# A two-block cross-attention kernel: the second block's context read from a kept transpose

## The reference, cut to what matters

```python
# first block, on x
x = attn(ln(x, g1, b1), ln(x, g1, b1), Wq1, Wk1, Wv1, Wo1, bo1) + x      # SELF
x = attn(ln(x, g2, b2), context, Wq2, Wk2, Wv2, Wo2, bo2) + x            # CROSS
x = geglu_ff(ln(x, g3, b3), Wp, bp, Wf, bf) + x                          # GEGLU
# second block
q, k, v = x @ Wq + bq, context @ Wk + bk, context @ Wv + bv              # CROSS2
out = softmax(q * 8**-0.5 @ k.T) @ v @ Wo + bo
out = out + gelu(ln(out) @ W1 + b1) @ W2 + b2                            # FFN
return x + out
```

## Time and profile before

| what | value |
| --- | --- |
| median of three runs | 463.78 us |
| lowest and highest run | 463.76 us, 464.13 us |
| profiled execution, its own time | 464.39 us |
| its span, first to last instruction | 462.7 us |
| TensorE matmul, weight load | 448.1 us (97%), 408.1 us (88%) |
| VectorE, ScalarE, GpSimd | 354.1, 322.5, 199.0 us |
| mean granted TensorE clock | 1.000 |

### The profile page before, as it was taken

One profiled execution on the slowest core, in us unless ns is written; L12 is line 12 of the kernel. 1 busy time (PEld: TensorE's weight loads), 2 busy tenths in 40 slices (PEclk: granted clock), 3 DMA queues, 4 the chain that ended last, 5 costly groups with the idle time before them and its releaser, 6 DMA issues.

```text
span 462.7 us, 17536 instructions
## 1 busy us (share of the span) xinstructions
PE 448.1 (97%) x7574; PEld 408.1 (88%) x7574; DVE 354.1 (77%) x642; ACT 322.5 (70%) x598; POOL 199.0 (43%) x219
## 2 busy tenths in 40 slices
PE   7989999999999999999999999999999999999897
PEld 6969898898998989989889899898999787777797
DVE  4899778778786787877877778696885678889572
ACT  5676776877778768877787777855545577776763
POOL 2584432555354634544353433531442232132583
PEclk9999999999999999999999999999999999999999
DMA  7102020310200000000000000000000000000011
GB/s 225 35 23 64 22 81 3 77 47 4 61 4 12 1 11 11 3 11 1 13 11 1 11 3 11 2 3 3 1 0 10 18 10 20 0 2 1 10 37 47
DMA packets 17301, 10.57 MB, mean 23 GB/s; under 512 B 7888, under 2 KB 16272, under 8 KB 17232
## 3 DMA queue, kind: packets, MB, share of 16 engines
q1 hardware_dynamic: 16800, 9.48, 7.4%
q10 hardware_dynamic: 432, 0.07, 0.1%
HBM read 8.50 MB, written 1.05 MB: 21 GB/s over the span
## 4 chain that ended last, share of the span: by engine, by line
PE 85%; DVE 9%; ACT 3%; issue 1%; DMA 1%; POOL 1%; DVEq 0%; SPq 0%
PE stage L606 12%; PE stage L608 11%; PE stage L607 11%; PE scp L697 7%; PE scp L772 7%; PE scp L921 6%; PE scp L742 6%; PE out0p L792 4%; PE out0p L818 3%; PE out0p L793 3%; PE out0p L794 3%; PE stage L756 2%; PE scp L713 2%; PE stage L621 1%; DMA pr<-in_L_xattn_Wq_dram 1%
## 5 line engine op out<-in xcount | busy, mean ns | idle before, releaser
L1464 POOL TENSOR_TENSOR pr<-pr,rc 128x1024 f32<-128x1024 f32 x32 | 60.2, 1903 | 71.3 <-DVE rc L1255 71.3
L1007 ACT ACTIVATE pr<-pr 128x1024 f32<-128x1024 f32 x48 | 50.7, 1056 | 34.4 <-DVE pr L1225 26.5
L1405 POOL TENSOR_TENSOR rstd<-veps,neghalf 128x2 f32<-128x2 f32 x32 | 22.4, 700 | 85.6 <-DVE veps L1173 85.4
L945 ACT ACTIVATE vt<-stage 64x512 f32<-64x512 f32 x80 | 47.3, 591 | 11.4 <-PE stage L608 8.9
L1220 DVE TENSOR_REDUCE mx<-scp 128x16 f32<-128x1024 f32 x32 | 39.2, 1224 | 11.5 <-PE scp L697 11.0
L1273 DVE COPY pt<-scp 128x512 f32<-128x512 f32 x32 | 22.1, 692 | 32.0 <-PE scp L742 31.8
L1268 DVE TENSOR_TENSOR ot_r<-scp,ot_h 128x512 fp32r<-128x512 f32 x64 | 41.1, 685 | 6.0 <-ACT ot_h L945 4.4
L945 ACT ACTIVATE ot_h<-scp 128x512 fp32r<-128x512 f32 x64 | 34.8, 598 | 12.5 <-PE scp L772 12.5
L945 ACT ACTIVATE q_of_heads<-stage 128x512 f32<-128x512 f32 x62 | 35.3, 596 | 10.2 <-PE stage L608 8.4
L945 ACT ACTIVATE k_of_heads<-stage 128x512 f32<-128x512 f32 x62 | 37.1, 600 | 5.4 <-PE stage L608 0.3
L1253 DVE TENSOR_REDUCE sm<-pr 128x16 f32<-128x1024 f32 x32 | 38.7, 1210 | 2.4 <-ACT pr L1007 2.4
(11 more groups left out here) (254 smaller groups left out, 1408.7 us busy)
## 6 DMA issues: line engine op xcount, KB each, us to landing
ctx_in<-in_ctx_dram SPq DMA_DIRECT2D x16, 96.0 KB, 2.0
masked_k<-in_L_xattn_Wo_dram SPq DMA_DIRECT2D x2, 512.0 KB, 4.2
out_dram<-rows SPq DMA_DIRECT2D x8, 128.0 KB, 1.8
rows<-in_x_dram SPq DMA_DIRECT2D x1, 768.0 KB, 9.3
pr<-in_L_xattn_Wq_dram SPq DMA_DIRECT2D x1, 512.0 KB, 4.8
pr<-in_L_xattn_Wk_dram SPq DMA_DIRECT2D x1, 512.0 KB, 6.4
pt<-in_L_xattn_Wv_dram SPq DMA_DIRECT2D x1, 512.0 KB, 7.6
rows<-in_L_xattn_Wq_dram SPq DMA_DIRECT2D x1, 512.0 KB, 3.7
```

The source lines that it names most:

```text
L945: return nc.scalar.activation(dst, s, ACT.Copy)
L1007: nc.scalar.activation(pr[t][:, :], pr[t][:, :], ACT.Exp, scale=scale[s.phase]).then_inc(exped, 1)
L1464: nc.gpsimd.tensor_tensor(halves(pr[t][:, :]), halves(pr[t][:, :]), rc[:, t, :, None].to_broadcast([ROWS, H, N]), ALU.mult).then_inc(probs, 1)
```

## The change: what it does

The transposed context of each group is no longer put into the two buffers cT. CROSS writes it into rows2, 256 columns of 96 partitions for each of the eight groups, where it stays until CROSS2. The q/k and v products of CROSS2 read it there. Group g's output in CROSS2 is written to the same columns of rows2 after the products of group g have read them. The eight context loads, sixteen transposes and eight copies of CROSS2 are left out. CROSS2 is written out in full on all engines that go through each_group. And x_step of two is put ahead of the v product of one in CROSS2, in the program and in the count of the banks, so that the nine uses are pt2, pt3, qk, x, v, pt0, pt1, at, wo: now x and pt1 share a bank, and v, pt3 and at share another.

```diff
-WITH_CTX = (CROSS, CROSS2)
@@ Counts.x
-        if p in WITH_CTX:
+        if p == CROSS:
             self.tick(f"ctx{g % 2}", (p, g), 16)
             self.tick("ctx_turned", (p, g))
@@ Counts.group
                 self.qk(p, g + 1)
-                self.use("v", p, g + 1)
                 if two.phase == CROSS2:
                     self.x(two.phase, two.first)
+                self.use("v", p, g + 1)
@@ tiles
-        cT = [sb(f"cT{n}", [C, GR]) for n in range(2)]
@@ each_group
-                if p in (SELF, CROSS):
+                if p in (SELF, CROSS, CROSS2):
                     for g in range(GROUPS):
                         body(Step(p, g))
                     continue
-                lead, tail = (2 if p == CROSS2 else 0), (4 if looks_far and p in (GEGLU, FFN) else 2)
-                for g in range(lead):
-                    body(Step(p, g))
-                turns = (GROUPS - tail - lead) // 2
+                tail = 4 if looks_far else 2
+                turns = (GROUPS - tail) // 2
                 with eng.Fori(0, turns) as turn:
-                    body(Step(p, lead, turn, turns))
-                    body(Step(p, lead + 1, turn, turns))
+                    body(Step(p, 0, turn, turns))
+                    body(Step(p, 1, turn, turns))
+        def turned_ctx(s):
+            return rows2[0:C, s.first * GR:(s.first + 1) * GR]
@@ context loads of SyncE
-            for p in WITH_CTX:
-                for g in range(2):
-                    if p == CROSS2:
-                        sp.wait_ge(ctx_turned, cnt.at("ctx_turned", Step(CROSS, GROUPS - 2 + g)))
-                    load_ctx(Step(p, g))
...
+            for g in range(2):
+                load_ctx(Step(CROSS, g))
...
@@ TensorE x_step
-                if s.phase in WITH_CTX:
+                if s.phase == CROSS:
@@ TensorE qk_step and v_step
-                nc.tensor.matmul(bank[:, GR:2 * GR], wk1[:, :], cT[s.parity][:, :], start=True, stop=True)\
+                nc.tensor.matmul(bank[:, GR:2 * GR], wk1[:, :], turned_ctx(s), start=True, stop=True)\
...
-                                                cT[s.parity][:, b * N:(b + 1) * N],
+                                                turned_ctx(s)[:, b * N:(b + 1) * N],
@@ TensorE group, CROSS2
                     if not last:
-                        v_step(one, s)
                         if two.phase == CROSS2:
                             x_step(two, s)
+                        v_step(one, s)
                     cross2_turn_step(s, 0)
@@ ScalarE x_turned_step
-                if s.phase in WITH_CTX:
-                    last = copy(cT[s.parity][:, :], bank[0:C, GR:2 * GR])
+                if s.phase == CROSS:
+                    last = copy(turned_ctx(s), bank[0:C, GR:2 * GR])
```

More of the change, by code:

```diff
@@ L541, in load_ctx @@
                              c[:, bass.ds(step.at(T), T), :]).then_inc(ctx_loaded[step.parity], 16)
-            for p in WITH_CTX:
+            for g in range(2):
+                load_ctx(Step(CROSS, g))
+            with sp.Fori(0, GROUPS // 2 - 1) as turn:
                 for g in range(2):
-                    if p == CROSS2:
-                        sp.wait_ge(ctx_turned, cnt.at("ctx_turned", Step(CROSS, GROUPS - 2 + g)))
-                    load_ctx(Step(p, g))
-                with sp.Fori(0, GROUPS // 2 - 1) as turn:
-                    for g in range(2):
-                        sp.wait_ge(ctx_turned, cnt.at("ctx_turned", Step(p, g, turn, GROUPS // 2 - 1)))
-                        load_ctx(Step(p, g + 2, turn, GROUPS // 2 - 1))
+                    sp.wait_ge(ctx_turned, cnt.at("ctx_turned", Step(CROSS, g, turn, GROUPS // 2 - 1)))
+                    load_ctx(Step(CROSS, g + 2, turn, GROUPS // 2 - 1))
             o = out.rearrange("b n d -> (b n) d").rearrange("(t p) d -> p t d", p=ROWS)
@@ L972, in x_high_step @@
                 if s.phase == CROSS:
-                    last = copy(ctx_src[s.parity][0][:, :], cT[s.parity][:, :])
+                    last = copy(ctx_src[s.parity][0][:, :], turned_ctx(s))
                 last.then_inc(high, 1)
@@ L1434, in rest_step @@
                     hp, rp = ctx_src[s.parity]
-                    last = nc.gpsimd.tensor_tensor(rp[:, :], cT[s.parity][:, :], hp.bitcast(F32)[:, :], ALU.subtract)
+                    last = nc.gpsimd.tensor_tensor(rp[:, :], turned_ctx(s), hp.bitcast(F32)[:, :], ALU.subtract)
                 last.then_inc(rest, 1)
```

## The result

The changed kernel takes 465.82 us (median of 7 runs, 465.14 to 466.24), the kernel before 464.13 in the same comparison. The ratio is 1.0034 with an interval of 1.0024 to 1.0044, so the change costs about 1.6 us. I had forecast 463.7, with a range up to 464.8, and the time lies above it. Times of the kernel before differ a little from one comparison to the next: 463.78 in the three runs that I forecast from, 464.13 here, 464.22 to 464.38 in the experiments.

What follows compares the result with a forecast made beforehand. The prediction took a closed chain of waits across TensorE, VectorE and ScalarE to bound CROSS2. Its terms, -0.27 + 0.10 + 0.05 = -0.12 us, gave 463.7 us, with a range from 462.7 to 464.8.

Steps and rivals of the forecast that it cites:

- The bound: In CROSS2 a closed chain of waits across engines, 8.33 us a group, sets the period, not TensorE's 97% busy share.
- the ring: CROSS2's chain from reciprocal through vb, max1, shift1, exp1, turn1, q/k products and out1 to the next reciprocal: 8.33 us.
- the rival that TensorE is the bound: In CROSS2 each of five groups gains 0.43 us, giving 461.4 us; chance 0.10.
- The two paths of the kernel before: In CROSS2, equally long paths from vb to turn1: one on TensorE, one on VectorE and ScalarE.
- First step, the context transposes: Two fewer transposes in each of CROSS2's groups 0 to 5 are worth 0; without cover, 0.43 us a group.
- Second step, x ahead of v: In CROSS2 groups 1 to 5 vb comes 0.02 us later: +0.10 us together, between 0 and +1.25.
- the slack: In CROSS2 the v product ends 0.27 us before VectorE starts vb, so it could be later by that much.
- the slower rival: In CROSS2 a late v product delays vb by 0.25 us in five groups: +1.0, 464.8 us; chance 0.08.
- Third step, the loop written out: Four CROSS2 groups leaving the loop cost 0.01 us each: +0.05 us together, between 0 and +0.28.
- Fourth step, the end of GEGLU: Context transposes leaving GEGLU groups 6 and 7 start CROSS2's first scores earlier: -0.27 us, between -0.22 and -0.57.
- Fifth step: Eight cT copies, eight context loads and other work off the path in CROSS2 and CROSS count 0.
- The third rival, a stall of straight code: One instruction stall in CROSS2's written-out code gives 463.7 + 1.5 = 465.2 us; chance 0.06.

Runs made afterwards that it cites:

- experiments 1: The changed kernel with the v product ahead of x again, kept context and written-out groups staying: 464.57 us, ratio 1.0008.
- experiment 3: The kernel before with only CROSS2's four looped groups written out: 464.75 us, ratio 1.0008.
- experiment 9: The changed kernel with v ahead of x again and the double waits before shift1 and turn1's first load made single: 463.49 us, ratio 0.9976.
- 11: The kernel before with CROSS2 written out and the double waits before shift1 and turn1's first load made single: 463.98 us, ratio 0.9996.
- experiment 12: The changed kernel with v first, single waits, and in groups 1 to 5 the k product moved behind v, beside x: 462.77 us, ratio 0.9965.
- experiment 2: The kernel before with only x_step, holding both the context and x pairs of transposes, put ahead of v: 466.83 us, ratio 1.0051.
- experiments 5: The changed kernel with v ahead of x again and two unused transposes with 128 weight columns ahead of v: 466.19 us, ratio 1.0040.
- 6: The changed kernel with v ahead of x again and two unused transposes with 64 weight columns ahead of v: 466.02 us, ratio 1.0032.
- experiment 7: The changed kernel with v ahead of x again and two unused ordinary narrow, alternating products ahead of v: 464.38 us, ratio 0.9998.

## Why the prediction was wrong, by its own steps

**The bound: right.** Taking ten transposes out of five groups changes the period by nothing while v goes first (experiments 1 and 3, 8.43 in both; 9 and 11, 8.30 in both). There TensorE waits for vb behind them, so this alone shows only that the wait covers them. In the changed kernel the cover is gone, and TensorE still stands idle for 0.43 us ahead of the scores, released by shift1. And taking 0.43 us out of the ring changes the period by 0.22 (experiment 12), until TensorE is full. So the rival that TensorE is the bound is refuted, and the page's 97% was indeed no guide. The two paths of the kernel before are as close as I read them: from the scores to turn1 it takes 1.06 to 1.11 us in the loop, where 1.04 to 1.05 is the least in any trace.

**First step, the context transposes: right, at 0, with v first.** In the changed order they would have stood ahead of v and cost 0.21 us a group: vb is 1.19 us after the reciprocal with them (experiment 2) and 0.98 without. The change's first part thus repaired some of the harm of its second.

**Second step, x ahead of v: this step failed, by its size.** I priced the pair at its pitch of 0.21 us and thus put vb 0.02 us later. v is later by 1.41 - 0.95 = 0.46 us, and vb by 0.25, after the slack is used. The pitch was read where the pair stands between other transposes. Behind out1 and ahead of v the pair costs 0.09 us in front and 0.16 behind on top (1.04 instead of 0.95, 0.37 instead of 0.21). The order costs 5 x 0.26 = 1.3 us, where the term in my sum was 0.10.

The mechanism stood in the text as the slower rival, and its sign came true: VectorE idle ahead of vb, released by the v product. That its bound of 0.25 us was met to the hundredth is luck. I had worked it out from the pitch of two pairs, 0.47 us, and one pair costs 0.46 here; with two pairs ahead of v it is 1.62 - 0.95 = 0.67 (experiment 2). I gave the rival 0.08, because I took the nearest row of the same instruction and not that of the same place. The kernel before has a pair of transposes ahead of such products:

```profile
387.69 1.11 PE L818 MATMUL out0p<-vb,pt 128*64 128x18 f32 x32
...
390.98 0.38 PE L829 MATMUL stage<-ident,att 128*128 128x128 f32 x2
391.29 1.19 PE L818 MATMUL out0p<-vb,pt 128*64 128x18 f32 x32
```

The pitch is 0.31 us there, from 390.98 to 391.29. Put in place of 0.21, it makes vb 0.09 us later: a part of the 0.25 could be read beforehand, not the whole. And by my own count x alone used up the slack to 0.01 us, which should have moved the chance.

**Third step, the loop written out: the cause right, its size wrong.** I wrote that of the 0.07 us from max1 to shift1 little comes out at the reciprocal. In the groups 2 to 5 it comes out in full: from shift1 to the next reciprocal it takes 5.48 us in experiments 1 and 3, and 5.46 to 5.49 in the loop. In group 1, which had this loss already, it was hidden by a quicker turn1. That turn1 stands in group 2's part of the program, in the loop, and its first load follows exp1's end at 377.39 by 0.05 us:

```profile
377.44 0.85 PEld L756 LDWEIGHTS stage<-ident,pr 128*128 128x128 f32 x8 [0.42 <-ACT pr L1007]
```

In the other looped groups this gap is 0.08 to 0.12 us, and wherever turn1 of the groups 1 to 5 is written out with two waits it is 0.10 to 0.12. So group 1 too goes from 8.36 to 8.42. The five groups together take 42.12 us in experiments 1 and 3 and 41.76 before: the cost is 0.36 us, where I took 0.05 and had 0.28 as the upper bound. The page "Runtime: NRT & Kernel Launch" of the Trainium skill, section "Instruction fetch mechanics", lets one expect that straight code gains over a loop; experiment 3 shows 464.75 us against 464.22 for the loop, no gain.

**Fourth step, the end of GEGLU: right at its lower bound.** Group 6 of GEGLU takes 4.87 us instead of 5.08, 0.21 us. The second pair is worth nothing, for the scores start 0.15 us after the masked keys in both kernels (359.28 to 359.43, and 359.40 to 359.55): the keys already set the start, and the 0.05 us that I allowed for their semaphore was too little. I had taken 0.27. The first scores come only 0.12 us earlier in the trace, since that execution was 0.08 us behind before this stretch (343.88 against 343.80).

**Fifth step: right at 0.** The loads and copies lay off the path.

The sum with the measured sizes is 1.31 + 0.36 - 0.21 = 1.46 us. In the two traces the reciprocal of group 6's start is later by 415.44 - 413.89 = 1.55 us, of which 0.08 was there before. The measured ratio of 1.0034 is 1.6 us. The rest of the distance to the forecast of 463.7 is the start: the kernel before took 464.13 us in this comparison and not 463.78. My range was also narrower than my own bounds: 463.78 + 1.25 + 0.28 - 0.22 is 465.1, not 464.8. The third rival, a stall of straight code, is not seen: the added idle time of VectorE and of the matmuls has a releaser, and the longest without one among the weight loads of CROSS2 is 0.53 us, less than the 0.70 before.

## What to carry to other kernels

Where two paths of equal length meet, work removed from one is worth nothing, and work moved ahead of a result that the other waits for is paid at once; look for the result's reader before moving anything ahead of it. Price a moved instruction from a row with the same neighbours, not from a row of the same instruction. When a forecast rests on slack of a few hundredths of a microsecond, give the other side a chance that fits.

## What the runs showed of the hardware that I had not expected

Two transposes between narrow products that alternate between partition halves made the second row of them 0.46 us later with 128 columns of weights and 0.43 with 64, where the pitch of the wide pair between other transposes is 0.21 (experiments 5 and 6). Two ordinary narrow, alternating products in the same place cost 0.14 (experiment 7). With two pairs ahead it was 0.67 us, 0.20 more than their pitches of 0.47 (experiment 2): the price on top came about once, not once a pair.

In the written-out code an instruction with two waits on different semaphores in front of it, whose later one had just been met, started about 0.05 to 0.07 us later than with one (experiment 9: shift1 1.33 and 1.26 us after max1, turn1's load 0.11 and 0.06 after exp1). Where both were met long before, at max1, nothing was lost. In the loop, where the counts come from registers, shift1 shows no such delay, but turn1 mostly does. Why this is so no run shows.
